# Attention and FFN in one kernel: the hand-over to the FFN re-ordered, with tile 0's reload in four transfers

## The chip, the core and the metric

One Trainium2 chip, one core. The time is the device time of one execution in microseconds, as the median of the runs. The core has TensorE (PE), VectorE (DVE), ScalarE (ACT), GpSimd (POOL) and SyncE (SP), which issues nearly all transfers here. Each engine runs its own program in order; they wait for one another on semaphores.

## What is computed

x has the shape (8, 1024, 512), the context (8, 64, 384); all is float32. Cut to its core:

```python
h = layernorm(x)                                   # over 512 channels, no gain
q, k, v = h @ Wq + bq, ctx @ Wk + bk, ctx @ Wv + bv   # 16 heads of 32
a = softmax(clip(q k^T * 32**-0.5, -1e4, 1e4))     # 64 keys
a = where(any(isnan(a)), 1/64, a)
x = x + (a v) @ Wo + bo
h = layernorm(x) @ W1 + b1                         # 2048 hidden channels
imag = w_imag * sin(theta + 0.1 * h)
h = h + 0.1 * (cos(theta) * w_real + sin(theta) * w_imag) * imag
x = x + relu(h) @ W2 + b2
```

## The kernel before, in words

The 8192 tokens are cut into 16 tiles of 512 (`TILES`), each of four blocks of 128 rows (`NB`). Every engine's program is written out by hand, with a `wait_ge` ahead of each operation that needs another engine. Most products are split: a float32 operand is held as a rounded part (`..._hi`) and the rest (`..._lo`), and `product` issues three matmuls (hi*hi, lo*hi, hi*lo; L1129 to L1131). ACT writes the hi part out of PSUM, DVE subtracts it to get the lo part.

**Phase A, attention.** The loop over `i` (0 to `STEPS_A` - 1 = 69) takes a group of four heads of a tile per step; there are 64 groups (`GROUPS`), four to a tile. At step i PE makes the scores of group i, transposes the probabilities of group i - 2 (`late = i - LAG_A`, L1198 to L1213, into the banks `pt_bank`), makes the queries of group i + 1, one output block y of `n = i - 6` (attention output times Wo, bank `y_bank`) and then the product of probabilities and values of group `late` (bank `o_bank`). Behind the scores of a group stands a chain over three engines: DVE clips (L983) and takes the maximum, POOL subtracts it (L591), ACT takes the exponential, POOL adds halves, DVE sums and inverts, POOL multiplies by the inverse (L586, `prob_done`). The steps 64 to 69 only drain: the last transposes at 64 and 65, the blocks y 58 to 63 at 64 to 69. For each block DVE adds the residual that SP has loaded into `res` (L1039, `y_done`), and SP stores it to the buffer `x1_dram` (L423), then loads the residual three blocks further on (L427) as soon as the store of the block that used the same quarter of `res` has landed. At step 64 PE also makes one small product (L1317), which counts rows without NaN; DVE casts it (`nan_count`), and POOL decides by it and sets `guard_done` (L620), on which SP's reload of finished rows waits.

**The seam.** SP loads tiles 0 and 1 of the attention's result back into `x_sb[0]` and `x_sb[1]` (L437 to L438), inside its loop over the blocks, behind the load for block 60. POOL adds `bo_row` block by block (`add_output_bias`, L555), DVE takes the statistics (`layer_stats`, two blocks at step 67, two at step 68), POOL takes the power -1/2 (`rsqrt`, L521), DVE makes the shifts (`layer_shift`, L869, at step 69), ACT normalises the four blocks into `xn` (L690), PE transposes them (L1135 in `transposes`, into banks 0 to 3), ACT and DVE split the result into `xt_hi` and `xt_lo` (L673, L875), and PE begins the FFN. Ahead of these transposes PE waits for all 64 residual additions (`y_done`, L1336).

**Phase B, FFN.** For each tile 16 hidden chunks f: PE makes the hidden values (banks 0 to 3), ACT, DVE and POOL work out the sine and the activation, PE multiplies chunk f - 3 by W2 into banks 4 to 7 (`second`). In tile 0 ACT and DVE also split the rest of the weights; before the first of these splits they wait until all blocks of `x1_dram` are stored and POOL has set `last_done`. The hidden chunk 1 and those after it follow one another on ACT and DVE through `turns`, `frac`, `hid` and `act`.

Of the kernel before, what the change touches and what calls it, by code (L numbers as in the profile page):

```python
# [15 lines left out]
P = 128  # L16
# [56 lines left out]
def ring(at):  # L73
    return 2 + at % 6
# [15 lines left out]
def y_bank(i):  # L90
    return ring(STEP_AT[i % KC] + 3 + KC * (i % KC == 2))
# [20 lines left out]
def xattn_ffn(nc, x, ctx_768, wq, bq, wk, bk, wv, bv, wo, bo, w1, b1, phases, w_real, w_imag, w2, b2,  # L112
# [6 lines left out]
    with stack:  # L119
# [123 lines left out]
        x0_in = sems("x0_in", NB)  # L243
# [60 lines left out]
        def x_loads(T):  # L304

            return 16 * ((T + 1) // XBUFS)
# [66 lines left out]
        def _(sp):  # L373
# [46 lines left out]
            for n in range(TILES * NB):  # L420
# [13 lines left out]
                if n == NB * GUARDED + 1:  # L434
                    sp.wait_ge(guard_done, 1)
                    sp.wait_ge(xt_psum, KC * TILES)
                    for t in range(XBUFS):  # L437
                        sp.dma_start(x_sb[t][:], x1_rows[t]).then_inc(x_in[t], 16)  # L438
# [41 lines left out]
        def _(pool):  # L480
# [69 lines left out]
            def add_output_bias(t, n):  # L550
                tile = x_sb[t % XBUFS]
                pool.wait_ge(x_in[t % XBUFS], x_loads(TILES + t))
                if t == 0 and n == 0:
                    pool.wait_ge(bias_in, 48)
                pool.tensor_tensor(tile[:, n, :], tile[:, n, :], bo_row[:], ALU.add).then_inc(x1_whole, 1)  # L555
# [68 lines left out]
            rsqrt(TILES)  # L624
            for n in range(NB):
                add_output_bias(1, n)
# [32 lines left out]
        def _(act):  # L659
# [15 lines left out]
            def layer_rows(T, blocks):  # L675
                if T == TILES or T < TILES:
                    if T:
                        act.wait_ge(x_in[T % XBUFS], x_loads(T))
# [167 lines left out]
        def _(dve):  # L846
            def layer_stats(T, blocks):
                if T:
                    dve.wait_ge(x_in[T % XBUFS], x_loads(T))
# [107 lines left out]
            for i in range(STEPS_A):  # L957
# [73 lines left out]
                if i in (STEPS_A - 3, STEPS_A - 2):  # L1031
                    layer_stats(TILES, half_blocks(i - STEPS_A + 3))
                if i == STEPS_A - 1:
                    layer_shift(TILES)
# [90 lines left out]
        def _(pe):  # L1125
# [52 lines left out]

            for i in range(STEPS_A):
# [16 lines left out]
                if 0 <= late < GROUPS:  # L1196

                    pe.wait_ge(prob_done, late + 1)  # L1198
                    for j in range(PAIRS):
                        if late == 0:  # L1200
                            pe.wait_ge(vn_done, 3) if j else pe.wait_ge(kt_done, 1)
                        elif has_burst(i - 1):
                            pe.wait_ge(xt_lo_done, KC * (t + 1) + j + 1)
                        elif j == 0 and late >= 2:
                            pe.wait_ge(o_lo_done, late - 1)
                        else:
                            pe.wait_ge(pt_lo_done, PAIRS * late - 1)
                        for blk in range(NB):
                            heads = slice(blk * HG + 2 * j, blk * HG + 2 * j + 2)
                            m = pe.transpose(psum[:, pt_bank(i, j), blk * P:(blk + 1) * P],  # L1210
                                             prob[:, late % SCORE_BUFS, heads, :].rearrange("p h k -> p (h k)"),
                                             ident[:])
                        m.then_inc(pt_psum, 1)  # L1213
# [54 lines left out]
                if 0 <= n < TILES * NB:  # L1268
# [3 lines left out]
                    if i < GROUPS:  # L1272
                        if g < 2:
                            pe.wait_ge(q_full_done, i + 1)
                        elif g == 2:
                            pe.wait_ge(pt_lo_done, PAIRS * (late + 1))
                    elif i == GROUPS + LAG_A:
# [10 lines left out]
                    m.then_inc(y_psum, 1)  # L1288
                if 0 <= late < GROUPS:
# [30 lines left out]
            def second(j):  # L1320
                t, f = divmod(j, FC)
                if t == 0:
                    pe.wait_ge(w_lo_done, w2_split[f])
                pe.wait_ge(act_lo_done, j + 1)
# [11 lines left out]
            pe.wait_ge(y_done, NB * TILES)  # L1336
# [57 lines left out]
```

## Time and profile before

| | before |
|---|---|
| median of 3 runs | 2078.79 us (2077.18 to 2079.24) |
| the profiled execution: its time, its span | 2078.33 us, 2076.6 us |
| TensorE's mean granted clock | 0.998 of full speed |
| PE busy | 2049.5 us (99%) |
| DVE, ACT, POOL busy | 1354.3, 1145.1, 1041.6 us |

The span is the stretch that the profile covers; the execution's time is 1.7 us more. Times in the rows are microseconds from the start of the span. A row's busy time of a matmul reaches until its result is out, so that matmuls which follow without a pause overlap: the starts of two neighbours, not their busy times, tell what one costs.

### The profile page before, as it was taken

To read this page: it belongs to the slowest core of one execution; us is meant where nothing else is said; L and a number is where in the kernel's file an instruction comes from. 1 tells how busy PE (TensorE), PEld (TensorE's weight loads), DVE (VectorE), ACT (ScalarE), POOL (GpSimd) and SP (SyncE) were. 2 spreads that over 40 slices of the span, in tenths; PEclk is the share of its full clock that TensorE was granted. 3 is DMA by queue.
4 is the path that set the end of the run, shared out by engine and by line. 5 is a ranking of instruction groups with operands and counts; after the bars stand their busy time and mean duration, and the time that the engine had idled before them with its cause. 6 is when DMAs were issued, how large, how long until landed. Compare 5 with 4: busy or idle time off the path is not lost.

```text
span 2076.6 us, 27122 instructions
## 1 busy us (share of the span) xinstructions
PE 2049.5 (99%) x9746; PEld 1715.9 (83%) x9746; DVE 1354.3 (65%) x2024; ACT 1145.1 (55%) x2036; POOL 1041.6 (50%) x757
## 2 busy tenths in 40 slices
PE   7999999999998999999999999999999999999999
PEld 5888888888887888888888888888888888888887
DVE  5888888888876665555555565555656555565554
ACT  4767667666664655454554545544455454554543
POOL 3777777777775245343343533435334353343521
PEclk9999999999999999999999999999999999999999
DMA  5123222222213221211112111121111211112100
GB/s 183 56 78 111 82 94 100 87 102 87 72 52 128 88 71 49 72 41 41 41 51 71 41 41 41 51 72 41 41 41 51 71 41 41 41 46 77 40 22 21
DMA packets 133462, 133.93 MB, mean 64 GB/s; under 512 B 68680, under 2 KB 84552, under 8 KB 133328
## 3 DMA queue, kind: packets, MB, share of 16 engines
q1 hardware_dynamic: 132176, 131.64, 21.2%
q8 instruction: 77, 1.26, 0.3%
q10 hardware_dynamic: 1152, 0.56, 0.1%
q14 instruction: 57, 0.47, 0.1%
HBM read 81.83 MB, written 50.35 MB: 64 GB/s over the span
## 4 chain that ended last, share of the span: by engine, by line
PE 89%; DVE 4%; ACT 2%; issue 2%; DMA 1%; POOL 1%; SPq 0%; POOLq 0%; ACTq 0%; DVEq 0%
PE psum L1129 28%; PE psum L1131 28%; PE psum L1130 28%; PE psum L1210 2%; PE psum L1135 1%; DVE hid L1061 1%; DMA ctx_sb<-in_ctx 0%; DVE prob L983 0%; DVE act_lo L1064 0%; ACT act_hi L813 0%; DMA x_sb<-in_x 0%; DVE top L989 0%; DVE total L969 0%; ACT hid L824 0%; POOL prob L591 0%
## 5 line engine op out<-in xcount | busy, mean ns | idle before, releaser
L642 POOL TENSOR_TENSOR frac<-turns,frac 128x512 f32<-128x512 f32 x256 | 333.4, 1302 | 830.0 <-DVE frac L1089 830.0
L1061 DVE SCALAR_TENSOR_TENSOR hid<-frac,gain,hid 128x512 f32<-128x512 f32 x256 | 322.4, 1259 | 143.6 <-ACT frac L809 142.4
L1129 PE MATMUL psum<-w_hi,act_hi 128*128 128x512 f32 x1024 | 398.4, 389 | 0.9 <-DVE act_lo L1064 0.9
L1130 PE MATMUL psum<-w_lo,act_hi 128*128 128x512 f32 x1024 | 398.3, 389 | 0.0
L1131 PE MATMUL psum<-w_hi,act_lo 128*128 128x512 f32 x1024 | 398.3, 389 | 0.0
L813 ACT ACTIVATE act_hi<-hid 128x512 fp32r<-128x512 f32 x256 | 161.8, 632 | 356.3 <-DVE hid L1061 356.3
L822 ACT ACTIVATE turns<-psum,u_shift 128x512 f32<-128x512 f32 x256 | 176.5, 689 | 327.1 <-PE psum L1131 268.9
L1064 DVE SCALAR_TENSOR_TENSOR act_lo<-hid,act_hi 128x512 fp32r<-128x512 f32 x256 | 197.6, 772 | 178.8 <-ACT act_hi L813 178.8
L1089 DVE TENSOR_SCALAR frac<-turns 128x512 f32<-128x512 f32 x256 | 111.3, 435 | 249.0 <-ACT turns L822 249.0
L1129 PEld LDWEIGHTS psum<-w_hi,act_hi 128*128 128x128 f32 x1024 | 192.3, 188 | 41.2 <-issue 1.2
L1131 PEld LDWEIGHTS psum<-w_hi,act_lo 128*128 128x128 f32 x1024 | 192.2, 188 | 40.0
L1130 PEld LDWEIGHTS psum<-w_lo,act_hi 128*128 128x128 f32 x1024 | 192.1, 188 | 39.8
L1129 PE MATMUL psum<-xt_hi,w1a_hi 128*128 128x512 f32 x512 | 199.6, 390 | 0.0
L1130 PE MATMUL psum<-xt_lo,w1a_hi 128*128 128x512 f32 x512 | 199.4, 389 | 0.0
L1131 PE MATMUL psum<-xt_hi,w1a_lo 128*128 128x512 f32 x512 | 199.2, 389 | 0.0
L1129 PE MATMUL psum<-xt_hi,w1b_hi 128*128 128x512 f32 x512 | 199.2, 389 | 0.0
L1130 PE MATMUL psum<-xt_lo,w1b_hi 128*128 128x512 f32 x512 | 199.2, 389 | 0.0
L1131 PE MATMUL psum<-xt_hi,w1b_lo 128*128 128x512 f32 x512 | 199.2, 389 | 0.0
L586 POOL TENSOR_TENSOR prob<-prob,inv 128x1024 f32<-128x1024 f32 x64 | 122.0, 1906 | 105.5 <-DVE inv L971 105.5
L824 ACT ACTIVATE hid<-psum,par 128x512 f32<-128x512 f32 x256 | 174.5, 682 | 0.0
L809 ACT ACTIVATE frac<-frac 128x512 f32<-128x512 f32 x256 | 161.3, 630 | 0.0
L748 ACT ACTIVATE psum<-psum 128x512 f32<-128x512 f32 x128 | 74.5, 582 | 122.5 <-DVE prob L983 122.5
(149 smaller groups left out, 4178.6 us busy)
## 6 DMA issues: line engine op xcount, KB each, us to landing
res<-in_x SPq DMA_DIRECT2D x64, 256.0 KB, 2.9
x_dram<-res SPq DMA_DIRECT2D x64, 256.0 KB, 2.0
x_sb<-x_dram SPq DMA_DIRECT2D x16, 1024.0 KB, 5.5
x_sb<-in_x SPq DMA_DIRECT2D x15, 1024.0 KB, 5.8
xn<-turn_dram SPq DMA_DIRECT2D x30, 512.0 KB, 5.1
out<-x_sb SPq DMA_DIRECT2D x15, 1024.0 KB, 4.9
turn_dram<-stage SPq DMA_DIRECT2D x112, 128.0 KB, 2.4
stage<-in_w SPq DMA_DIRECT2D x32, 256.0 KB, 2.8
```

Of the source, the lines that this page charges most:

```text
L586: pool.tensor_tensor(rows, rows, inv[:, (i - 1) % 2, :].unsqueeze(2) .to_broadcast([P, NB * HG, KEYS]), ALU.mult).then_inc(prob_done, 1)
L642: pool.tensor_tensor(frac[:, j % 2, :], turns[:, j % 2, :], frac[:, j % 2, :], ALU.subtract)\
L809: act.activation(frac[:, j % 2, :], frac[:, j % 2, :], ACT.Sin, scale=SIN_SCALE).then_inc(sin_done, 1)
L813: act.activation(act_hi[:, j % ACTS, :], hid[:, j % 2, :], ACT.Relu).then_inc(act_hi_done, 1)
L822: act.activation(turns[:, j % 2, :], hidden, ACT.Identity, bias=u_shift[:, f:f + 1], scale=0.1 / TWO_PI).then_inc(turns_done, 1)
L824: act.activation(hid[:, j % 2, :], hidden, ACT.Identity, bias=par[:, 3, f:f + 1])\
L1061: dve.scalar_tensor_tensor(out=hid[:, j % 2, :], in0=frac[:, j % 2, :], scalar=gain[:, f:f + 1], in1=hid[:, j % 2, :], op0=ALU.mult, op1=A ...
L1064: dve.scalar_tensor_tensor(out=act_lo[:, j % ACTS, :], in0=hid[:, j % 2, :], scalar=0.0, in1=act_hi[:, j % ACTS, :].bitcast(F32), op0=ALU. ...
L1089: dve.tensor_scalar(frac[:, j % 2, :], turns[:, j % 2, :], ROUND, ROUND, ALU.add, ALU.subtract)\
L1129: pe.matmul(o, a_hi, b_hi, start=first, stop=False)
L1130: pe.matmul(o, a_hi, b_lo, start=False, stop=False)
L1131: return pe.matmul(o, a_lo, b_hi, start=False, stop=last)
```

## The change

Six edits, all around the seam:

1. The transposes of the probabilities become a function `transpose_rows(i)`. Those of the last group (63) are called at step 64 behind the block y, no longer at step 65 ahead of it. Their waits are the same.
2. Block y of step 62 (n = 56) goes to bank 5, no longer to bank 7, and waits there for `o_lo_done` of group 59; before, it waited for both lo parts of the probabilities of group 60 (`pt_lo_done`).
3. Tile 0's reload is four transfers of a block each, with four semaphores `x1_in`; POOL adds the bias to a block when that block is in. ACT and DVE need no wait of their own for this load, and have none.
4. DVE takes the statistics of all four blocks and the shifts at step 67, ahead of the residual additions of blocks 61, 62 and 63.
5. POOL waits for these shifts before it adds the bias to tile 1.
6. PE's wait for `y_done` moves from ahead of the first FFN transposes to ahead of the first product with W2.

```diff
 def y_bank(i):
-    return ring(STEP_AT[i % KC] + 3 + KC * (i % KC == 2))
+    return ring(STEP_AT[i % KC] + 3 + (2 if i == GROUPS - 2 else KC) * (i % KC == 2))
...
-            return 16 * ((T + 1) // XBUFS)
+            return 16 * ((T + 1) // XBUFS - (T >= TILES and T % XBUFS == 0))
...
-                    for t in range(XBUFS):
-                        sp.dma_start(x_sb[t][:], x1_rows[t]).then_inc(x_in[t], 16)
+                    for blk1 in range(NB):
+                        sp.dma_start(x_sb[0][:, blk1, :], x1_rows[0][:, blk1, :]).then_inc(x1_in[blk1], 16)
+                    sp.dma_start(x_sb[1][:], x1_rows[1]).then_inc(x_in[1], 16)
...
             def add_output_bias(t, n):
                 tile = x_sb[t % XBUFS]
-                pool.wait_ge(x_in[t % XBUFS], x_loads(TILES + t))
+                if t:
+                    pool.wait_ge(x_in[t % XBUFS], x_loads(TILES + t))
+                else:
+                    pool.wait_ge(x1_in[n], 16)
...
             rsqrt(TILES)
+            pool.wait_ge(shift_rows_done, TILES + 1)
             for n in range(NB):
                 add_output_bias(1, n)
...
-                if T == TILES or T < TILES:
-                    if T:
-                        act.wait_ge(x_in[T % XBUFS], x_loads(T))
+                if 0 < T < TILES:
+                    act.wait_ge(x_in[T % XBUFS], x_loads(T))
...
-                if T:
+                if T and T != TILES:
                     dve.wait_ge(x_in[T % XBUFS], x_loads(T))
...
-                if i in (STEPS_A - 3, STEPS_A - 2):
-                    layer_stats(TILES, half_blocks(i - STEPS_A + 3))
-                if i == STEPS_A - 1:
+                if i == STEPS_A - 3:
+                    layer_stats(TILES, range(NB))
                     layer_shift(TILES)
...
-                if 0 <= late < GROUPS:
-
-                    pe.wait_ge(prob_done, late + 1)
...
+                if 0 <= late < GROUPS - 1:
+                    transpose_rows(i)
...
-                        elif g == 2:
+                        elif has_burst(i):
                             pe.wait_ge(pt_lo_done, PAIRS * (late + 1))
+                        elif i == GROUPS - 2:
+                            pe.wait_ge(o_lo_done, late)
...
+                if i == GROUPS:
+                    transpose_rows(i + 1)
                 if 0 <= late < GROUPS:
...
+                if j == 0:
+                    pe.wait_ge(y_done, NB * TILES)
                 pe.wait_ge(act_lo_done, j + 1)
...
             pe.wait_ge(nan_count, 1)
-            pe.wait_ge(y_done, NB * TILES)
             pe.wait_ge(xn_done, TILES + 1)
```

How the instructions stand on the engines. PE in step 64 and at the start of step 65, before; `pt`, `vbd` is the product with the values, `row_ok` the NaN count, `wo` a block y, and `[waits ...]` names the semaphores:

```order
L1131 MATMUL psum<-wo_hi,o_lo 128x512
L1129 MATMUL psum<-pt_hi,vbd_hi 128x512 [waits pt_lo_done,y_done]
L1130 MATMUL psum<-pt_lo,vbd_hi 128x512
L1131 MATMUL psum<-pt_hi,vbd_lo 128x512
L1129 MATMUL psum<-pt_hi,vbd_hi 128x512 [waits pt_lo_done]
L1130 MATMUL psum<-pt_lo,vbd_hi 128x512
L1131 MATMUL psum<-pt_hi,vbd_lo 128x512
L1317 MATMUL psum<-ones,row_ok 1x1 [waits nan_step]
L1210 MATMUL psum<-ident,prob 128x128 [waits o_lo_done,prob_done]
L1210 MATMUL psum<-ident,prob 128x128 x3
L1210 MATMUL psum<-ident,prob 128x128 [waits pt_lo_done]
L1210 MATMUL psum<-ident,prob 128x128 x3
```

The same place after the change:

```order
L1134 MATMUL psum<-wo_hi,o_lo 128x512
L1197 MATMUL psum<-ident,prob 128x128 [waits o_lo_done,prob_done]
L1197 MATMUL psum<-ident,prob 128x128 x3
L1197 MATMUL psum<-ident,prob 128x128 [waits pt_lo_done]
L1197 MATMUL psum<-ident,prob 128x128 x3
L1132 MATMUL psum<-pt_hi,vbd_hi 128x512 [waits pt_lo_done,y_done]
L1133 MATMUL psum<-pt_lo,vbd_hi 128x512
L1134 MATMUL psum<-pt_hi,vbd_lo 128x512
L1132 MATMUL psum<-pt_hi,vbd_hi 128x512 [waits pt_lo_done]
L1133 MATMUL psum<-pt_lo,vbd_hi 128x512
L1134 MATMUL psum<-pt_hi,vbd_lo 128x512
L1328 MATMUL psum<-ones,row_ok 1x1 [waits nan_step]
```

The eight transposes of the last group now stand ahead of the six matmuls with the values of group 62 and of the NaN count.

DVE from step 66 to the FFN's first lo parts, before; `res` is a residual addition (blocks 60 to 63), `mv` and `var_eps` end the statistics:

```order
L1039 TENSOR_TENSOR res<-psum,res 128x512
L857 BN_STATS stats<-x_sb0 128x6 x2
L1039 TENSOR_TENSOR res<-psum,res 128x512
L857 BN_STATS stats<-x_sb0 128x6 x2
L861 BN_AGGR mv<-stats 128x2 x4
L864 TENSOR_SCALAR var_eps<-mv 128x4
L1039 TENSOR_TENSOR res<-psum,res 128x512
L869 SCALAR_TENSOR_TENSOR shift_rows<-mv,rstd 128x4
L1039 TENSOR_TENSOR res<-psum,res 128x512
L875 TENSOR_TENSOR xt_lo<-psum,xt_hi 128x512 x4
```

After the change:

```order
L1042 TENSOR_TENSOR res<-psum,res 128x512
L861 BN_STATS stats<-x_sb0 128x6 x4
L865 BN_AGGR mv<-stats 128x2 x4
L868 TENSOR_SCALAR var_eps<-mv 128x4
L873 SCALAR_TENSOR_TENSOR shift_rows<-mv,rstd 128x4
L1042 TENSOR_TENSOR res<-psum,res 128x512 x3
L879 TENSOR_TENSOR xt_lo<-psum,xt_hi 128x512 x4
```

Three residual additions that stood between and behind the statistics now stand behind the shifts.

SP's issues around the reload; `x_sb0` and `x_sb1` are tiles 0 and 1, and the rows around them the store and the load of the blocks in the loop:

```order
@@ -155,6 +155,6 @@
 L423 DMA x1_dram<-res 128x512
 L427 DMA res<-in_x 128x512
-L438 DMA x_sb0<-x1_dram 128x4x512
-L438 DMA x_sb1<-x1_dram 128x4x512
+L438 DMA x_sb0<-x1_dram 128x512 x4
+L439 DMA x_sb1<-x1_dram 128x4x512
 L423 DMA x1_dram<-res 128x512
```

One issue has become four, so the store of block 58 and all behind it on this queue stand three issues further back.

## Rows read from the trace of the kernel before

**Rows 1.** PE at the seam, timeline: start, busy, operation [idle before] (us)
```profile
637.87 0.50 PE L1129 MATMUL psum<-wo_hi,o_hi 128*128 128x512 f32 x1 [0.92 <-DVE pt_lo L995]
...
653.54 0.47 PE L1129 MATMUL psum<-pt_hi,vbd_hi 128*128 128x512 f32 x1 [0.59 <-DVE pt_lo L995]
...
655.20 1.09 PE L1210 MATMUL psum<-ident,prob 128*128 128x128 f32 x8
...
670.89 0.39 PE L1131 MATMUL psum<-wo_hi,o_lo 128*128 128x512 f32 x1
675.62 3.18 PE L1135 MATMUL psum<-ident,xn 128*128 128x128 f32 x16 [4.34 <-ACT xn L690]
...
679.73 0.39 PE L1129 MATMUL psum<-xt_hi,w1a_hi 128*128 128x512 f32 x1
```

**Rows 2.** The timeline of DVE at the seam
```profile
663.23 0.69 DVE L1039 TENSOR_TENSOR res<-psum,res 128x512 f32<-128x512 f32 x1 [1.47 <-PE psum L1131]
...
667.61 0.69 DVE L1039 TENSOR_TENSOR res<-psum,res 128x512 f32<-128x512 f32 x1 [2.34 <-DMA res<-in_x]
...
669.53 0.38 DVE L861 BATCH_NORM_AGGREGATE mv<-stats 128x2 f32<-128x6 f32 x4
...
671.25 1.22 DVE L869 SCALAR_TENSOR_TENSOR shift_rows<-mv,rstd 128x4 f32<-128x4 f32 x1 [0.53 <-POOL rstd L521]
...
679.47 0.69 DVE L875 TENSOR_TENSOR xt_lo<-psum,xt_hi 128x512 fp32r<-128x512 f32 x1 [0.16 <-ACT xt_hi L673]
```

**Rows 3.** The timeline of POOL at the seam
```profile
652.41 1.91 POOL L586 TENSOR_TENSOR prob<-prob,inv 128x1024 f32<-128x1024 f32 x1 [1.09 <-DVE inv L971]
656.22 0.10 POOL L620 MEMSET ones<- 128x1 f32 x1 [1.90 <-DVE ok_count L1030]
662.00 5.04 POOL L555 TENSOR_TENSOR x_sb<-x_sb,bo_row 128x512 f32<-128x512 f32 x4 [5.68 <-DMA x_sb<-x_dram]
670.19 1.02 POOL L521 TENSOR_TENSOR rstd<-var_eps,minus_half 128x4 f32<-128x4 f32 x1 [3.15 <-DVE var_eps L864]
```

**Rows 4.** The timeline of ACT at the seam
```profile
642.28 0.60 ACT L796 ACTIVATE o_hi<-psum 128x512 fp32r<-128x512 f32 x1 [2.67 <-PE psum L1131]
...
672.55 2.93 ACT L690 ACTIVATE xn<-x_sb,shift_rows,rstd 128x512 f32<-128x512 f32 x4 [9.88 <-issue]
```

**Rows 5.** The timeline of SP, which issues the transfers
```profile
656.35 0.93 SPq L438 DMA_DIRECT2D x_sb<-x_dram  x2
...
666.03 0.33 SPq L427 DMA_DIRECT2D res<-in_x  x1
...
668.20 0.33 SPq L427 DMA_DIRECT2D res<-in_x  x1
```

**Rows 6.** The loads of x_sb (L438), then of res (L427): issue to landing
```profile
DMA to landing us min/median/max: 5.6/7.1/8.6
...
DMA to landing us min/median/max: 2.8/2.9/9.7
```

**Rows 7.** The windows behind the long wait: busy us by engine, PEclk, DMA
```profile
675.60:680.00 4.40, 4.38 (x21) 4.12 (x22) 2.61 (x4) 2.39 (x4) 0.57 (x2) 0.61 0.11 33
```

**Rows 8.** The chain that ended last, from FFN tile 0 to tile 1
```profile
684.44 0.24 PE psum L1131
684.71 0.69 ACT turns L822
...
764.58 0.47 PE psum L1129
```

**Rows 9.** The program's first microseconds, with tile 0's four loads
```profile
0.80 1.81 SPq L397 DMA_DIRECT2D x_sb<-in_x  x4
...
9.34 0.69 DVE L857 BATCH_NORM_STATS2 stats<-x_sb 128x6 f32<-128x512 f32 x1 [1.27 <-DMA x_sb<-in_x]
...
11.87 0.16 DVE L869 SCALAR_TENSOR_TENSOR shift_rows<-mv,rstd 128x4 f32<-128x4 f32 x1 [1.22 <-POOL rstd L521]
```

More of the change, by code:

```diff
@@ L242, in xattn_ffn @@
         x_in = sems("x_in", XBUFS)
-        x0_in = sems("x0_in", NB)
+        x0_in, x1_in = sems("x0_in", NB), sems("x1_in", NB)
         res_in, x1_stored = sems("res_in", NB), sems("x1_stored", NB)
@@ L1177, in _, with transpose_rows @@
             values(0)
+            def transpose_rows(i):
+                t, late = i // KC, i - LAG_A
+                pe.wait_ge(prob_done, late + 1)
+                for j in range(PAIRS):
+                    if late == 0:
+                        pe.wait_ge(vn_done, 3) if j else pe.wait_ge(kt_done, 1)
+                    elif has_burst(i - 1):
+                        pe.wait_ge(xt_lo_done, KC * (t + 1) + j + 1)
+                    elif j == 0 and late >= 2:
+                        pe.wait_ge(o_lo_done, late - 1)
+                    else:
+                        pe.wait_ge(pt_lo_done, PAIRS * late - 1)
+                    for blk in range(NB):
+                        heads = slice(blk * HG + 2 * j, blk * HG + 2 * j + 2)
+                        m = pe.transpose(psum[:, pt_bank(i, j), blk * P:(blk + 1) * P],
+                                         prob[:, late % SCORE_BUFS, heads, :].rearrange("p h k -> p (h k)"),
+                                         ident[:])
+                    m.then_inc(pt_psum, 1)
             for i in range(STEPS_A):
@@ L1195, in _ @@
                             m.then_inc(s_psum, 1)
-                if 0 <= late < GROUPS:
-                    pe.wait_ge(prob_done, late + 1)
[L1199 to L1213, printed above, removed]
+                if 0 <= late < GROUPS - 1:
+                    transpose_rows(i)
                 if i + 1 < GROUPS:
```

## The prediction

> **What bounds the kernel now.** I read the page first. PE is busy for 99% of the span and the other engines for at most 65%, and the chain that ended last lies on PE for most of its length, so only time in which PE stands still or runs slowly can be won. Then PE's timeline, for its pauses. The largest within the program is the seam: the last matmul of the last block y starts at 670.89, and the first FFN transpose starts at 675.62, behind a wait of 4.34 us for ACT's `xn` [rows 1]. Behind it PE is slow as well. The window from 675.60 to 680.00 has a granted clock of 0.61, a mean of its two levels, 2.4 GHz (1.00) and 1.2 GHz (0.50), and the second trio of FFN products (the first matmul that runs at the full pace again) starts at 679.73, so 16 transposes and three matmuls took 4.11 us [rows 1, 7]. Two smaller pauses lie ahead of it: 0.92 us in front of block y 56, and 0.59 us in front of the values of group 62, both for `pt_lo` [rows 1].
>
> Then what is late at the seam, backwards. ACT normalises from 672.55, for 2.93 us [rows 4]. It waits for DVE's shifts, which start at 671.25 and take 1.22 us; these wait for POOL's power (670.19, 1.02 us) and this for the statistics, whose last part starts at 669.53 [rows 2, 3]. The statistics are late because DVE stood for 2.34 us, until 667.61, in front of a residual addition whose load had not landed [rows 2]. POOL's four bias additions run from 662.00 to 667.04, behind a wait of 5.68 us for the reload that SP issued at 656.35 [rows 3, 5]. So two things make `xn` late: a reload that counts only as a whole, and residual additions ahead of the statistics in DVE's order.
>
> **The tail of attention (edits 1 and 2).** Block y 56 no longer waits for `pt_lo`; the group 59 that it now waits for is two groups back. PE is 0.92 us ahead from there. The softmax chain of group 63 follows, since ACT's copy in front of it waited for PE (2.67 us idle, until 642.28) [rows 4]. POOL's last multiplication, 652.41 + 1.91 = 654.32, thus ends at 653.40 [rows 3]. PE reaches the moved transposes when block y 58 is issued: 653.54 - 0.59 = 652.95 before, 652.03 now [rows 1]. It waits there for the probabilities, 653.40 - 652.03 = 1.37 us. Removed are 0.92 + 0.59 = 1.51, added 1.37: I take a gain of 0.1. Bounds: if POOL's chain doesn't move up, PE waits 2.29 and loses 0.8; if the pause were hidden it would gain 1.5. It is a trade of one stall for another, because the probabilities aren't there earlier.
>
> Queued behind the moved transposes are the values of group 62 and the NaN count. Eight transposes cost some 0.9 (busy 1.09 with the result's way out [rows 1]), so these values start near 654.4, where they started at 653.54, and the count with them is 0.8 to 0.9 later. On the count hang `guard_done` (656.22) and the reload (656.35) [rows 3, 5]: it goes out at about 657.2. This is the price of edit 1 for the seam. The values of group 63 have 0.2 us to spare by my count of ACT's and DVE's copies (0.6 to 0.7 us each, one behind the other, under the 12 matmuls of block y 59); a miss costs a few tenths.
>
> **The seam (edits 3, 4, 5).** A transfer of 256 KB of the same shape takes 2.8 to 2.9 us where nothing is in its way [rows 6], so the first quarter lands at 657.2 + 2.9 = 660.1. POOL's four additions, 5.04 us [rows 3], then end at 665.1, if the other quarters come at least every 1.26 us, the last by 663.9. The whole first megabyte took 5.6 us [rows 6], which would be 662.8, plus what three more issues of 0.47 us cost [rows 5]; so they should. DVE is free after block 60's addition at 663.23 + 0.69 = 663.9 [rows 2]. The fourth statistics end at 665.1 + 0.7 = 665.8, the rest of them at 666.4 (0.38 us [rows 2], and a small addition), POOL's power at 667.5 (1.02 [rows 3]), the shifts at 667.7, ACT at 667.7 + 2.93 = 670.7 [rows 4]. PE's last block y is issued by 670.89 + 0.23 - 0.1 = 671.0 [rows 1, 8]. `xn` comes 0.3 ahead of that: the pause closes. The transposes start at 671.1, where they started at 675.62.
>
> The shifts took 1.22 us beside POOL's additions for tile 1, and 0.16 us at the start of the program [rows 2, 9]; edit 5 keeps POOL still, and I take 0.2. If they still took 1.22, `xn` would be ready at 671.7 and 0.3 to 0.7 us would be lost. The Trainium skill (GPSIMD Engine Reference, Specifications) says that GpSimd's SBUF interfaces are shared with VectorE, with contention for DVE instructions with two SBUF inputs, as this one has. By that rule it is the short one, by 1.06 us; the trace agrees.
>
> **What is late next.** Without the pause the clock has no reason in this trace to fall: it stood at full through pauses of 0.92 and 0.59 us and fell only behind the one of 4.34 [rows 1, 7]. At full pace 16 transposes take 1.75 (twice the eight) and three matmuls 0.68. But `xt_lo` now stands in DVE's queue behind three residual additions, of which the last needs the load of block 63. That load waited for a store and was issued at 668.20 [rows 5]; the bytes in front of it are the same and start 0.8 later, so 669.0, and it lands at 671.9. Addition and first `xt_lo` take 0.69 each [rows 2]: 673.3, and the trio behind them ends its issue at 674.0. That is 679.73 - 674.0 = 5.7 us earlier than before. Without the late load it would be 671.1 + 2.43 = 673.5, a gain of 6.2; with the slow clock nevertheless, 671.1 + 4.11 = 675.2, a gain of 4.5.
>
> **Is it kept?** From 684.71 to 764.58 the chain that ended last runs over ACT and DVE, not PE: the first FFN tile, in which they split weights too [rows 8]. It hangs on PE's hidden chunk 1, issued at 684.44 [rows 8], so it starts earlier with PE, by the same 5.7. Two things in it don't hang on PE. The last block must be stored: added by 672.6, landed near 676. POOL must have passed `last_done`: four additions behind the shifts, 667.7 + 5.0 = 672.7. ACT asks for both some 1.6 us before `turns` of chunk 1 (two copies of weights of about 0.6 us, and a short pause), so at 684.7 - 5.7 - 1.6 = 677.4. Both are in, the store with about 1 us to spare. Behind tile 0 nothing changes. Edit 6 by itself costs nothing: by the first product with W2 all additions are long over.
>
> **Sum.** 0.1 + 4.4 (pause) + 1.2 (clock, less the late load) = 5.7 us. The profiled execution took 2078.33, 1.7 more than its span, and goes to 2072.6; the median of the runs lies 0.46 above that execution, so 2073.1.
>
> **The rivals.**
>
> *The quarters come late.* At the start of the program four such quarters were issued from 0.80 on, and the statistics of the fourth waited until 9.34, 8.5 us [rows 9]; other loads followed close behind, as here tile 1's megabyte does. So the last quarter lands at 665.8, its bias ends at 667.1, `xn` at 672.7. The pause is 1.7, the gain 2.9 plus up to 1.7 of clock: 2074.2 to 2075.9. At the worst the four land together with the last, 657.2 + 5.6 + 1.4 = 664.2, and POOL's 5.04 follow: `xn` at 674.9, the gain 0.7, 2078.1. The Trainium skill speaks against the split (DMA: Bandwidth & Descriptors, Rules for kernel authors: at least 1 MiB per DMA for bandwidth); by it this rival is the case. For it speaks the start, against it the quiet queue ahead of this reload, and that 256 KB loads take 2.9. Chance 0.20, a third of it with a gain over 4.2.
>
> *The gain is lost behind the seam or in the tail.* The clock falls at the new pause of 1.4 us (a stretch of some 4 us at half pace costs 2), or the store of the last block holds the chain in tile 0. Gain 2.5 to 4: 2074.8 to 2076.3. Chance 0.11.
>
> *Slower.* The load of block 63 is now ahead of `xt_lo`. One load of `res` took 9.7 us [rows 6]. Issued at 669.0 that is 678.7, with 1.4 of DVE and 0.7 of PE 680.8, against 679.73 before: 1 us slower, 2079.9. It decides from a landing at 677.6 on. Against it: that load had two megabytes in front of it, which are through by 666. Chance 0.03; over 0.2% slower would need 4 us more, hence I leave 0.02 for that.
>
> *The forecast*, 2071.8 to 2074.5: chance 0.66.
>
> **How the numbers follow.** 0.2% is 4.2 us, about what a measurement of this kernel can tell. Faster by more: 0.66 and a third of 0.20, 0.72. Slower 0.02, the same 0.26. The range goes from 2071.6 (the gain of 6.2 and some more in the tail) to 2076.5, which takes in the late quarters and most of the losses.
>
> **What would show it.** Block y 56 starts straight behind the queries. The transposes of group 63 wait near 1.4 us for POOL. POOL's first bias addition begins near 660 and has no long pauses after it. The shifts take about 0.2 and come before three additions. The FFN's transposes have no pause over 0.5 in front, and the granted clock behind them is full. The first `xt_lo` comes near 672.6. The prediction is wrong if POOL waits between its four additions, if PE's clock is under full at 654 or 672, or if the chain in tile 0 begins at something other than PE.

## The result, and the profile after

| | before | changed |
|---|---|---|
| median of 11 runs | 2077.4 us (2075.13 to 2079.24) | 2072.85 us (2071.2 to 2075.03) |
| ratio to before, 95% interval | | 0.998 (0.9971 to 0.9989) |
| the profiled execution: time, span | 2078.33, 2076.6 us | 2072.03, 2070.3 us |
| PE busy | 2049.5 us | 2047.8 us |

The change makes the kernel faster by 0.2%: 4.2 us by the ratio (2.3 to 6.0), 4.55 us by the medians. The forecast was 2073.1 us, a gain of 5.7.

The two profiled executions differ by 6.3 us of span, and not all of it is the change. The start of the program, which the change doesn't touch, happened to be quicker: the residual addition of block 55 on DVE starts at 630.64 before and at 629.99 after. So times of the two traces are compared as distances from this addition. Two distances are used from here on: to the first FFN transpose on PE (44.98 us before, 40.34 after), and to ACT's `turns` of hidden chunk 1, at which the chain through FFN tile 0 begins (54.07 before, 48.64 after); the recorded expectations call this second distance the yardstick. The seam is thus 5.43 us shorter; from `turns` of chunk 1 to the end of the span it is 1391.9 us before and 1391.7 after.

The timeline of PE in the changed kernel, around the seam (start, busy, operation, idle before), which answers to [rows 1]:

```profile
652.49 1.09 PE L1197 MATMUL psum<-ident,prob 128*128 128x128 f32 x8 [1.41 <-POOL prob L590]
...
669.89 0.39 PE L1134 MATMUL psum<-wo_hi,o_lo 128*128 128x512 f32 x1
670.33 1.94 PE L1138 MATMUL psum<-ident,xn 128*128 128x128 f32 x16
672.87 0.47 PE L1132 MATMUL psum<-xt_hi,w1a_hi 128*128 128x512 f32 x1 [0.61 <-DVE xt_lo L879]
...
673.65 0.39 PE L1132 MATMUL psum<-xt_hi,w1a_hi 128*128 128x512 f32 x1
```

The wait of 4.34 us for `xn` is gone; the transposes follow the last block y with no pause that the view lists. New are 1.41 us ahead of the moved transposes, for POOL's last multiplication, and 0.61 us ahead of the first FFN product, for the first `xt_lo`. The 16 transposes take 1.94 us instead of 3.18. A window over this stretch shows why (columns: the stretch, its length, busy time and count of PE, PEld, DVE, ACT and POOL, then the granted clock, the DMA share and GB/s):

```profile
671.00:674.00 3.00, 2.39 (x17) 2.01 (x16) 2.56 (x5) 2.06 (x4) 1.36 (x3) 1.00 0.68 255
```

It is at 1.00, 2.4 GHz, where [rows 7] had 0.61. The timeline of DVE, for [rows 2]:

```profile
662.23 0.69 DVE L1042 TENSOR_TENSOR res<-psum,res 128x512 f32<-128x512 f32 x1 [1.47 <-PE psum L1134]
662.83 2.46 DVE L861 BATCH_NORM_STATS2 stats<-x_sb 128x6 f32<-128x512 f32 x4
665.33 0.38 DVE L865 BATCH_NORM_AGGREGATE mv<-stats 128x2 f32<-128x6 f32 x4
...
667.05 0.16 DVE L873 SCALAR_TENSOR_TENSOR shift_rows<-mv,rstd 128x4 f32<-128x4 f32 x1 [1.13 <-POOL rstd L522]
667.95 0.69 DVE L1042 TENSOR_TENSOR res<-psum,res 128x512 f32<-128x512 f32 x1 [0.74 <-DMA res<-in_x]
...
671.43 0.69 DVE L1042 TENSOR_TENSOR res<-psum,res 128x512 f32<-128x512 f32 x1 [1.50 <-DMA res<-in_x]
672.04 2.47 DVE L879 TENSOR_TENSOR xt_lo<-psum,xt_hi 128x512 fp32r<-128x512 f32 x4
```

All four statistics run in one piece, the shifts take 0.16 us and start at 667.05, and only then the three residual additions come. The last of them, of block 63, waited 1.50 us for its load, and the first `xt_lo` stands right behind it. The statistics begin when DVE is done with block 60's addition, not when POOL is done: they end at 665.29, and POOL's last bias addition (below) ended at 664.01. POOL, for [rows 3]:

```profile
650.54 1.90 POOL L590 TENSOR_TENSOR prob<-prob,inv 128x1024 f32<-128x1024 f32 x1 [1.09 <-DVE inv L975]
656.04 0.10 POOL L624 MEMSET ones<- 128x1 f32 x1 [3.60 <-DVE ok_count L1034]
658.95 5.06 POOL L559 TENSOR_TENSOR x_sb<-x_sb,bo_row 128x512 f32<-128x512 f32 x4 [2.81 <-DMA x_sb<-x_dram]
666.00 1.02 POOL L522 TENSOR_TENSOR rstd<-var_eps,minus_half 128x4 f32<-128x4 f32 x1 [1.99 <-DVE var_eps L868]
```

POOL waits 2.81 us for the first quarter, where it waited 5.68 for the whole tile, and makes its four additions without a pause. ACT, for [rows 4, 8], and SP, for [rows 5]:

```profile
667.25 2.94 ACT L694 ACTIVATE xn<-x_sb,shift_rows,rstd 128x512 f32<-128x512 f32 x4 [5.58 <-DVE shift_rows L873]
...
678.63 0.69 ACT L826 ACTIVATE turns<-psum,u_shift 128x512 f32<-128x512 f32 x1 [0.41 <-PE psum L1134]
```

```profile
656.17 1.75 SPq L438 DMA_DIRECT2D x_sb<-x_dram  x4
...
668.63 0.33 SPq L427 DMA_DIRECT2D res<-in_x  x1
```

### The profile page after: what moved, and what is told of

Same layout as the page of the kernel before. It is cut to its first block, busy times and chain, and to the rows that moved or that the text cites. A ratio compares the mean times of both kernels' runs of the same rounds, so it can differ in the third digit from the quotient of the medians.

```text
span 2070.3 us, 27125 instructions
## 1 busy us (share of the span) xinstructions
PE 2047.8 (99%) x9746; PEld 1715.1 (83%) x9746; DVE 1353.3 (65%) x2024; ACT 1144.8 (55%) x2036; POOL 1041.0 (50%) x757
## 4 chain that ended last, share of the span: by engine, by line
PE 90%; DVE 4%; ACT 2%; DMA 1%; issue 1%; POOL 1%; SPq 0%; ACTq 0%; DVEq 0%; POOLq 0%
PE psum L1132 29%; PE psum L1134 29%; PE psum L1133 28%; PE psum L1197 2%; PE psum L1138 1%; DVE hid L1064 1%; DMA x_dram<-res 0%; DMA ctx_sb<-in_ctx 0%; ACT act_hi L817 0%; DVE act_lo L1067 0%; DMA x_sb<-in_x 0%; DVE prob L987 0%; ACT hid L828 0%; DVE top L993 0%; POOL prob L595 0%
```

## The experiments

Each experiment was profiled and timed against the kernel before on the same chip. A microsecond is 0.05%, less than the half-width of the intervals of the ratios (about 0.1%), so the small steps are read from the traces, by the two distances. Each distance is of one execution.

| run | block 55's addition | first FFN transpose | `turns` of chunk 1 | first distance | second distance | median, ratio (95% interval) |
|---|---|---|---|---|---|---|
| before | 630.64 | 675.62 | 684.71 | 44.98 | 54.07 | |
| changed | 629.99 | 670.33 | 678.63 | 40.34 | 48.64 | 2072.85, 0.998 (0.9971 to 0.9989) |
| e1: edit 1 undone | 630.61 | 670.11 | 678.06 | 39.50 | 47.45 | 2071.53, 0.9973 (0.9961 to 0.9984) |
| e11: the same again | 631.30 | 670.78 | 679.84 | 39.48 | 48.54 | 2071.53, 0.9977 (0.9966 to 0.9987) |
| e2: edit 3 undone | 628.21 | 670.83 | 679.87 | 42.62 | 51.66 | 2075.44, 0.9994 (0.9984 to 1.0003) |
| e3: edit 4 undone | 630.17 | 675.08 | 684.71 | 44.91 | 54.54 | 2077.33, 1.0003 (0.9994 to 1.0013) |
| e4: edit 6 undone | 629.44 | 672.93 | 680.87 | 43.49 | 51.43 | 2074.89, 0.9996 (0.9986 to 1.0006) |
| e5: edit 5 undone | 631.39 | 672.82 | 681.31 | 41.43 | 49.92 | 2071.05, 0.9976 (0.9964 to 0.9987) |
| e6: tile 1 loaded later | 627.77 | 668.16 | 677.87 | 40.39 | 50.10 | 2072.12, 0.9978 (0.9968 to 0.9988) |
| e7: first lo parts ahead of block 63 | 629.49 | 669.83 | 677.78 | 40.34 | 48.29 | 2071.83, 0.9976 (0.9966 to 0.9985) |
| e8: before, with edit 2 alone | 629.76 | 672.79 | 681.77 | 43.03 | 52.01 | 2075.18, 0.9992 (0.9983 to 1.0002) |
| e9: e1, NaN count earlier | 629.97 | 669.18 | 677.13 | 39.21 | 47.16 | 2070.28, 0.9968 (0.9956 to 0.9981) |
| e10: e9, part of block y 59 earlier | 627.69 | 666.43 | 674.35 | 38.74 | 46.66 | 2069.61, 0.9968 (0.9956 to 0.998) |
| e12: changed, NaN count earlier | 630.46 | 670.47 | 678.41 | 40.01 | 47.95 | 2071.32, 0.9972 (0.9962 to 0.9982) |

Of the experiments that undo an edit, only the interval of e3 (edit 4) lies clear of the changed kernel's; those of e2 and e4 overlap it slightly. For edits 1 and 5 the times show nothing: e1, e11 and e5 are as fast as the changed kernel or faster.

**e1 and e11: is edit 1 part of the gain?** The transposes of the last group go back to step 65:

```diff
-                if 0 <= late < GROUPS - 1:
+                if 0 <= late < GROUPS:
                     transpose_rows(i)
...
-                if i == GROUPS:
-                    transpose_rows(i + 1)
```

> The changed kernel with edit 1 undone: the transposes of the last group stand at step 65 again, ahead of block y 59; all else as changed. Yardstick for all experiments: from the start of the residual addition of block 55 on DVE to the start of ACT's turns of hidden chunk 1. Before 54.07 us, changed 48.64 us. Theory (edit 1 trades one stall for a longer one: PE stands 1.41 us for the probabilities where it stood 0.59 us for pt_lo): with it undone PE stands about 0.4 to 0.6 us in front of the values of group 62 and not at all in front of the transposes, the FFN's transposes come 0.8 to 0.9 us earlier, the reload 1.7 us earlier, yardstick 47.3 to 47.9. Rival (the move belongs to the gain, its cover for pt_lo is needed further on): yardstick 49.2 or more.

The timeline of PE in e1:

```profile
652.31 0.47 PE L1132 MATMUL psum<-pt_hi,vbd_hi 128*128 128x512 f32 x1 [0.63 <-DVE pt_lo L999]
...
653.97 1.09 PE L1197 MATMUL psum<-ident,prob 128*128 128x128 f32 x8
...
670.11 1.94 PE L1138 MATMUL psum<-ident,xn 128*128 128x128 f32 x16
672.30 0.47 PE L1132 MATMUL psum<-xt_hi,w1a_hi 128*128 128x512 f32 x1 [0.25 <-DVE xt_lo L879]
```

Two groups of heads behind each other, PE stands 0.63 us for `pt_lo`, and the transposes find their probabilities ready. The first distance is 0.84 us shorter, in both executions (39.50 and 39.48): 1.41 - 0.63 = 0.78 of it is this stall. The reload leaves SP 24.50 us behind block 55's addition (655.11 - 630.61), where it was 26.18 in the changed kernel, 1.7 us earlier. The theory holds for the stall. For the second distance (47.3 to 47.9 expected) it holds in e1, with 47.45, and not in e11, with 48.54:

> The kernel of the first experiment again, beside the two above on the same chip: yardstick 47.3 to 47.6, time 0.996 to 0.9985 of before.

The timeline of PE in e11, and DVE's addition of block 63 in e1 and in e11:

```profile
674.11 0.47 PE L1132 MATMUL psum<-xt_hi,w1a_hi 128*128 128x512 f32 x1 [1.39 <-DVE xt_lo L879]
```

```profile
670.42 0.69 DVE L1042 TENSOR_TENSOR res<-psum,res 128x512 f32<-128x512 f32 x1 [1.67 <-DMA res<-in_x]
```

```profile
672.67 0.69 DVE L1042 TENSOR_TENSOR res<-psum,res 128x512 f32<-128x512 f32 x1 [1.91 <-DMA res<-in_x]
```

The first FFN product waited 1.39 us for `xt_lo` here, 0.25 in e1, with the same instructions. The difference is the load of block 63, which was issued 1.25 us later (37.97 against 36.72 us behind block 55) and took 0.3 longer from issue to use (3.40 against 3.09). So edit 1 costs 0.84 us up to the transposes, in both executions. In the second distance its whole price, the stall and the later reload, is 1.19 us against e1 and only 0.10 against e11, where the load was as late as in the changed kernel (41.37 us behind block 55's addition, 41.44 there) although the reload had gone out earlier. By time the kernels can't be told apart: e1 and e11 have 0.9973 and 0.9977, the changed one 0.998.

**e2: what the four transfers are worth.**

```diff
-                    for blk1 in range(NB):
-                        sp.dma_start(x_sb[0][:, blk1, :], x1_rows[0][:, blk1, :]).then_inc(x1_in[blk1], 16)
+                    sp.dma_start(x_sb[0][:], x1_rows[0]).then_inc(x1_in[0], 16)
...
-                    pool.wait_ge(x1_in[n], 16)
+                    pool.wait_ge(x1_in[0], 16)
```

> The changed kernel with edit 3 undone: tile 0 is reloaded in one transfer of 1 MB, and POOL's four bias additions wait for it as a whole. Theory (the quarters let POOL begin 2.8 us after the issue, not 5.6): POOL begins 2.5 to 2.8 us later, the statistics end 2.2 us later, the FFN's transposes wait some 2 us for xn, yardstick 48.64 + 1.5 to 2.2 = 50.1 to 50.8, and up to 1.3 more if the granted clock falls behind this pause. Rival (the late load of block 63 in front of the first xt_lo sets the end anyway, the quarters give nothing): 48.6 to 49.0.

POOL and PE in e2, and a window behind PE's pause:

```profile
660.04 5.04 POOL L558 TENSOR_TENSOR x_sb<-x_sb,bo_row 128x512 f32<-128x512 f32 x4 [5.67 <-DMA x_sb<-x_dram]
```

```profile
670.83 3.54 PE L1137 MATMUL psum<-ident,xn 128*128 128x128 f32 x16 [2.33 <-ACT xn L693]
```

```profile
672.00:673.00 1.00, 1.00 (x7) 1.00 (x6) 0.36 (x1) 0.79 (x2) 0.82 (x2) 0.50 0.61 121
```

POOL waits 5.67 us again, PE 2.33, and the granted clock is 0.50 in the midst of the transposes, which take 3.54 us instead of 1.94. The second distance is 3.02 us longer: 2.28 in the pause (first distance), the rest the clock, less the late load, which the pause hides. The theory's figure with a fallen clock, 50.1 to 52.1, holds; the rival (48.6 to 49.0) is out.

**e3: the order on DVE.**

```diff
-                if i == STEPS_A - 3:
-                    layer_stats(TILES, range(NB))
+                if i in (STEPS_A - 3, STEPS_A - 2):
+                    layer_stats(TILES, half_blocks(i - STEPS_A + 3))
+                if i == STEPS_A - 1:
                     layer_shift(TILES)
```

> The changed kernel with edit 4 undone: two blocks' statistics at step 67, two at step 68, the shifts at step 69, with the residual additions between. Theory (the residual additions, which wait for loads behind the reload, held the statistics): the statistics end some 4 us later, the transposes wait 4 us for xn, yardstick 52.4 to 53.8, nearly the whole gain gone. Rival (the quarters alone made xn early, the order on DVE hardly matters): at most 49.6.

DVE and PE in e3:

```profile
668.17 0.69 DVE L1043 TENSOR_TENSOR res<-psum,res 128x512 f32<-128x512 f32 x1 [3.85 <-DMA res<-in_x]
```

```profile
675.08 3.65 PE L1139 MATMUL psum<-ident,xn 128*128 128x128 f32 x16 [4.60 <-ACT xn L694]
```

DVE stands 3.85 us in front of block 61's addition, with the second half of the statistics behind it, although the quarters came early. The second distance is 54.54, nothing left of the gain, 0.7 more than the theory's upper end: the load of block 61 is held by the reload and comes later than I had it. The quarters without the order are worth nothing, and the order without the quarters (e2) is worth 54.07 - 51.66 = 2.4 us, of which edit 2 alone gives 2.06 (e8, below). They need each other. Beside e8, which keeps the old reload and order, e3 is even 2.53 us slower: the load of block 61 is issued 3.0 us later (29.02 against 26.03 us behind block 55's addition), 1.7 of it since the reload goes out later, as edit 1 makes it do, and 1.3 since there are three more issues ahead of it on SP.

**e4: the wait for all additions ahead of the transposes.**

```diff
+            pe.wait_ge(y_done, NB * TILES)
             pe.wait_ge(xn_done, TILES + 1)
...
-                if j == 0:
-                    pe.wait_ge(y_done, NB * TILES)
```

> The changed kernel with edit 6 undone: PE waits for all 64 residual additions ahead of the first FFN transposes. Theory: the addition of block 63 ends 1.8 us behind the point at which the transposes can start now, so they start 1.9 us later; xt_lo stands behind the same addition anyway, so the hidden chunks come only about 1.3 us later: yardstick 49.8 to 50.1. Rival (edit 6 is worth nothing, since xt_lo has the same wait in DVE's order): 48.6 to 48.8.

PE in e4, and a window in its transposes:

```profile
672.93 1.94 PE L1138 MATMUL psum<-ident,xn 128*128 128x128 f32 x16 [3.19 <-DVE res L1042]
675.12 0.47 PE L1132 MATMUL psum<-xt_hi,w1a_hi 128*128 128x512 f32 x1 [0.25 <-DVE xt_lo L879]
```

```profile
673.00:674.00 1.00, 1.00 (x10) 1.00 (x11) 0.00 (x0) 0.34 (x1) 0.00 (x0) 1.00 0.31 117
```

The transposes start 3.15 us later, not 1.9, and `turns` 2.79 later, not 1.3. The direction is the theory's, the size for `turns` twice as large (51.43 against 49.8 to 50.1), and the rival (48.6 to 48.8) is out: the addition of block 63 came 42.70 us behind block 55's here, 41.44 in the changed kernel, so some 1.3 us of the 2.8 is the unsteady load. Edit 6 is worth 1.5 us with the load as it was in the changed kernel, more when the load is late. PE's pause of 3.19 us left the clock at 1.00, where the one of 2.33 in e2 brought it down.

**e5: POOL's wait for the shifts.**

```diff
-            pool.wait_ge(shift_rows_done, TILES + 1)
```

> The changed kernel with edit 5 undone: POOL goes on from the power to tile 1's bias additions without waiting for DVE's shifts. Theory (this small DVE instruction with two SBUF inputs is held while POOL's addition runs): the shifts take about 1.2 us instead of 0.16, the transposes start 1.0 us later, yardstick 48.64 + 0.4 to 0.6 = 49.0 to 49.3 since the late load of block 63 hides the rest. Rival (the 1.22 us before came of something else): shifts 0.16 to 0.3 us, yardstick 48.6.

DVE and POOL in e5:

```profile
668.46 1.25 DVE L872 SCALAR_TENSOR_TENSOR shift_rows<-mv,rstd 128x4 f32<-128x4 f32 x1 [1.13 <-POOL rstd L522]
```

```profile
668.40 5.00 POOL L559 TENSOR_TENSOR x_sb<-x_sb,bo_row 128x512 f32<-128x512 f32 x4
```

The shifts take 1.25 us again when POOL's additions start beside them, and the first distance grows by 1.09. The second grew by 1.28, above the 0.4 to 0.6 expected, since the load of block 63 was late here as well (42.72 us). The rival is out. The Trainium skill (GPSIMD Engine Reference, Specifications) names contention for DVE instructions with two SBUF inputs; this run agrees with it. The times don't show this loss: e5's median is 2071.05 us, and the profiled execution, with 2074.72, was the slowest of its seven.

**e6 and e7: the late load of block 63.** In e6 SP issues tile 1's reload behind the load of block 63; in e7 DVE makes the first `xt_lo` ahead of the addition of block 63.

```diff
-                    sp.dma_start(x_sb[1][:], x1_rows[1]).then_inc(x_in[1], 16)
+                if n == NB * GUARDED + 4:
+                    sp.dma_start(x_sb[1][:], x1_rows[1]).then_inc(x_in[1], 16)
```

```diff
                 if 0 <= n < TILES * NB:
+                    if n == TILES * NB - 1:
+                        for k in range(KC):
+                            xt_to_lo(TILES, k, k)
                     dve.wait_ge(res_in[n % NB], 16 * (n // NB + 1))
```

> The changed kernel, but SP issues the reload of tile 1 three blocks later, behind the load for block 63. Theory (the store of block 59 and so the load of block 63 were late because a megabyte for tile 1 stood ahead of them): this load lands before PE is done with block 63, PE's pause of 0.61 us in front of the first FFN product shrinks to about 0.1, yardstick 48.0 to 48.2; tile 1's bias additions begin near the time of the shifts or 1 to 2 us later and hold nothing. Rivals: the four quarters alone keep the stores back, 48.6; or tile 1's late bias additions hold last_done and with it the weight splits of the first FFN tile, 49 or more.

> The changed kernel, but DVE makes the four first xt_lo of the FFN ahead of the residual addition of block 63. Theory (only this addition, waiting for its load, kept the first xt_lo back): PE's pause of 0.61 us goes to about 0.1, yardstick 48.0 to 48.2; the store of block 63 goes out some 2.5 us later and is still in time for the weight splits, or just holds them (then 48.4 to 49). Rival (xt_lo is held by ACT's copies, not by the addition): 48.6.

PE and ACT in e6, then in e7:

```profile
670.35 0.47 PE L1133 MATMUL psum<-xt_hi,w1a_hi 128*128 128x512 f32 x1 [0.25 <-DVE xt_lo L880]
```

```profile
676.80 0.63 ACT L675 ACTIVATE w_hi<-stage 128x512 fp32r<-128x512 f32 x1 [2.14 <-POOL ones L642]
```

```profile
672.02 0.47 PE L1132 MATMUL psum<-xt_hi,w1a_hi 128*128 128x512 f32 x1 [0.26 <-DVE xt_lo L879]
```

```profile
676.52 0.64 ACT L674 ACTIVATE w_hi<-stage 128x512 fp32r<-128x512 f32 x1 [0.19 <-issue]
```

In both the pause in front of the first product is 0.25 us, so the rest of the 0.61 was the addition of block 63 and its load. In e6 tile 1's megabyte was late in turn: POOL passed `last_done` only at 676.51, ACT stood 2.14 us in front of the first weight split, and the second distance is 1.46 longer in spite of the earlier product, 50.10 where 48.0 to 48.2 was expected. That is the second rival. In e7 0.35 us are won; 48.29 is just above the 48.0 to 48.2 expected. ACT stands 0.19 us in front of the split there. The view names no releaser; POOL had passed `last_done` at 671.76, so most likely it is the store of block 63, the other thing that it waits for here.

**e8: edit 2 alone, on the kernel before.**

```diff
-    return ring(STEP_AT[i % KC] + 3 + KC * (i % KC == 2))
+    return ring(STEP_AT[i % KC] + 3 + (2 if i == GROUPS - 2 else KC) * (i % KC == 2))
...
-                        elif g == 2:
+                        elif has_burst(i):
                             pe.wait_ge(pt_lo_done, PAIRS * (late + 1))
+                        elif i == GROUPS - 2:
+                            pe.wait_ge(o_lo_done, late)
```

> The kernel before with edit 2 alone: block y 56 in bank 5, without its wait for pt_lo. Theory (the softmax chain of group 63 hangs on PE, so it moves up with it): the pauses of 0.4 and 0.59 us stay, everything behind comes 0.9 to 1.2 us earlier, the reload and all of the seam with it, yardstick 54.07 - 1.1 = 52.8 to 53.2. Rival (the chain over DVE, POOL and ACT keeps its own time and PE just waits elsewhere): 54.0.

PE in e8, and the starts around the pause of 0.92 us before:

```profile
651.44 0.47 PE L1129 MATMUL psum<-pt_hi,vbd_hi 128*128 128x512 f32 x1 [0.59 <-DVE pt_lo L995]
...
672.79 3.47 PE L1135 MATMUL psum<-ident,xn 128*128 128x128 f32 x16 [3.59 <-ACT xn L690]
```

```profile
636.56 0.39 PE L1131 MATMUL psum<-xt_hi,wq_lo 128*128 128x512 f32 x1
637.87 0.50 PE L1129 MATMUL psum<-wo_hi,o_hi 128*128 128x512 f32 x1 [0.92 <-DVE pt_lo L995]
638.21 0.40 PE L1130 MATMUL psum<-wo_lo,o_hi 128*128 128x512 f32 x1
```

The pause of 0.92 is gone and that of 0.59 is as long as it was, so the softmax chain follows PE, as the theory says. From block 55's addition to block 56's it is 9.13 us, where it was 10.35, so the pause had cost 1.22. The view counts it only from the end of the last result; by the starts, the two matmuls around it are 1.31 us apart where neighbours have 0.23, and the next one comes 0.34 behind. The second distance fell by 2.06, more than the 0.9 to 1.3 expected (52.8 to 53.2) and 0.84 more than the pause; the rest came in the seam, where block 61's addition waited 1.43 us for its load instead of 2.34.

**e9, e10 and e12: a better version.** The NaN count's product moves ahead of the values of group 62 (in e12, ahead of the moved transposes; in e9 with edit 1 undone); e10 also moves the first three matmuls of block y 59 there.

```diff
+                if i == GROUPS:
+                    pe.wait_ge(nan_step, 2)
+                    pe.matmul(psum[0:1, 0, 0:1], row_ok[:], ones[:], start=True, stop=True).then_inc(nan_psum, 1)
                 if 0 <= late < GROUPS:
...
-                if i == GROUPS:
-                    pe.wait_ge(nan_step, 2)
-                    pe.matmul(psum[0:1, 0, 0:1], row_ok[:], ones[:], start=True, stop=True).then_inc(nan_psum, 1)
```

In e10, in addition:

```diff
-                    for k in range(KC):
+                    for k in range(1 if i == GROUPS + 1 else 0, KC):
...
+                if i == GROUPS:
+                    slot, toks = (n + 1) // NB * KC % O_BUFS, slice((n + 1) % NB * P, ((n + 1) % NB + 1) * P)
+                    product(psum[:, y_bank(i + 1), :], (o_hi[:, slot, toks], o_lo[:, slot, toks]),
+                            (wo_hi[:, 0, :], wo_lo[:, 0, :]), True, False)
```

> The kernel of the first experiment (changed, edit 1 undone), and the NaN count's product ahead of the values of group 62, right behind block y 58. Yardsticks so far: before 54.07, changed 48.64, edit 1 undone 47.45. Theory (what is left of the seam is PE's own work, 0.25 us for the first xt_lo and some 0.2 us in front of the transposes, where xn is just late): the reload goes out 1.5 to 2 us earlier, xn is early, the loads of blocks 62 and 63 are early, yardstick 47.1 to 47.3. Rival (the pause for pt_lo moves, or DVE's order holds the count): 47.45 or more.

> The kernel of e9_count_up, and the first three matmuls of block y 59 (0.68 us) moved up a step into PE's pause of 0.6 us in front of the values of group 62. Theory: the pause goes, all behind it comes 0.6 us earlier, yardstick 0.5 to 0.6 less than that of e9_count_up, near 46.6. Rival: the values of group 63 then wait for their pt_lo, since block y 59 covers that wait with nine matmuls only, yardstick as e9_count_up.

> The changed kernel, edit 1 kept, with the NaN count's product ahead of the moved transposes. It parts the price of edit 1: the stall on PE (about 0.8 us) and the later reload. Theory: the reload goes out 3 to 3.9 us earlier, the load of block 63 is in time, PE's pause in front of the first FFN product shrinks from 0.61 to 0.25, yardstick 48.64 - 0.35 - 0.0 to 0.2 = 48.1 to 48.3; the rest to 47.45 is the stall. Rival (the late load of block 63 has nothing to do with the time of the reload): 48.6.

PE in e10, in e12, and POOL in e12:

```profile
651.02 1.04 PE L1197 MATMUL psum<-ident,prob 128*128 128x128 f32 x8
...
666.43 1.94 PE L1138 MATMUL psum<-ident,xn 128*128 128x128 f32 x16
668.62 0.47 PE L1132 MATMUL psum<-xt_hi,w1a_hi 128*128 128x512 f32 x1 [0.25 <-DVE xt_lo L879]
```

```profile
652.96 1.09 PE L1197 MATMUL psum<-ident,prob 128*128 128x128 f32 x8 [1.30 <-POOL prob L590]
...
672.67 0.47 PE L1132 MATMUL psum<-xt_hi,w1a_hi 128*128 128x512 f32 x1 [0.26 <-DVE xt_lo L879]
```

```profile
653.39 0.10 POOL L624 MEMSET ones<- 128x1 f32 x1 [0.49 <-issue]
656.30 5.07 POOL L559 TENSOR_TENSOR x_sb<-x_sb,bo_row 128x512 f32<-128x512 f32 x4 [2.80 <-DMA x_sb<-x_dram]
```

e12: the reload goes out 3.1 us earlier (653.52 - 630.46 = 23.06, after 26.18), the load of block 63 is in time, the pause in front of the first product is 0.26 and the second distance 47.95, a little under the 48.1 to 48.3 expected. Of the 0.69 us won, 0.35 is this pause; the other 0.33 is in the first distance, and block 60's addition is earlier by as much already (31.91 against 32.24 us behind block 55's), so it is won on PE and not by the reload. From e12 to e9 it is 0.79, the stall. e9 has 47.16 and e10 46.66, as expected: the view of PE shows no pause in front of the values of group 62 any more. e10's median is 2069.61, its ratio 0.9968 (0.9956 to 0.998), 6.6 us under the kernel before (4.2 to 9.1). Against the changed kernel the traces give 1.98 us; the intervals of the ratios (0.9956 to 0.998 and 0.9971 to 0.9989) overlap.

## Why the prediction was right

The time, the sign and the mechanism hold. The gain was forecast at 5.7 us; the traces of the two executions show 5.43 in the seam, the runs 4.2 (2.3 to 6.0). That the time itself was met to 0.25 us (2073.1 against 2072.85) is in part luck: the gain by medians was 1.15 us short of the forecast, and the kernel before has 2077.4 in eleven runs where the forecast set out from 2078.79 in three, 1.39 more. The times below are the prediction's, put on the changed execution's axis by taking off the 0.65 us that its start was quicker.

- **The tail.** POOL's last multiplication was to follow PE: it ends at 652.44 (forecast 652.75). PE was to stand 1.37 us for it; it stood 1.41. The removed pause was worth 1.22, not 0.92 (e8). The net gain in the tail is 0.35 us (the last matmul of block y: 669.89 + 0.65 = 670.54 against 670.89), not 0.1.
- **Edit 1 as a trade.** This step was the weakest. The prediction set the new stall against the sum of two old ones, 1.51 us, and found them nearly even. But edit 2 removes the one by itself, so edit 1 trades 0.6 us for 1.4, at a loss of 0.84 up to the transposes (e1, e11). Its other price, the later reload, was seen: 0.8 to 0.9 later than before was forecast; measured from block 55's addition it is 26.18 against 25.71 before, 0.5 later, since the tail in between gained.
- **The seam.** First bias addition at 659.5, shifts done at 667.1, `xn` done at 670.1, transposes at 670.5: measured 658.95, 667.21, 670.19, 670.33. The shifts took 0.16 us (0.2 taken), and e5 shows the cause. One link was other than forecast, and the errors happened to balance. The prediction let POOL's last addition set the end of the statistics; in the trace POOL was done 0.4 us ahead of the forecast, and DVE's own four statistics, which start right behind block 60's addition and take 2.46 us, set it. In all eight executions with edits 3 to 6 in place (the changed kernel, e1, e11, e6, e7, e9, e10, e12) the transposes start 8.10 to 8.13 us behind block 60's addition, whether the reload went out 23.1 or 26.2 us behind block 55's. So in the changed kernel the reload no longer sets the start of the transposes; in e2 it still does.
- **The clock.** Full behind the closed pause, as forecast; the transposes and the first trio took 673.65 - 670.33 = 3.3 us instead of 4.11. e2 shows the half clock behind a pause. The term of the sum for the clock, less the late load, was 1.2 us and came out at 5.43 - 4.64 = 0.79, since the forecast had only 2.9 us for this stretch. Its figure without the late load, 2.43, was too small as well: e1, with an early load, took 2.97 (670.11 to 673.08), for the first product waits 0.25 us for `xt_lo` there too. The tail and the pause were together 0.14 more than forecast (4.64 against 4.5).
- **What is late next.** The load of block 63 was forecast to be issued at 668.4 and to land at 671.3; it was issued at 668.63 and its addition started at 671.43. The first trio's end of issue, forecast 673.4, was 673.65. This is the most exposed step of the sum: in e3, e4 and e5 the addition of block 63 came 1.3 to 1.4 us later than in the changed kernel, and in e11 1.6 later than in e1, the same program, for reasons that these traces don't tell.
- **Kept through tile 0.** From `turns` of chunk 1 to PE's pause at the tile's end it is 79.63 us, after 79.87. The spare time of the two other conditions was real but thin: e6 and e7 used it up.
- **The rivals.** The quarters did not come like those at the start of the program; POOL had no pause between them, though pauses of 0.2 to 0.8 show in e5, e6 and e10. e2, with the megabyte whole, is 3.0 us slower in the seam; what counts here is when the first quarter can be used, not the rate. The rule of the Trainium skill (DMA: Bandwidth & Descriptors, Rules for kernel authors), at least 1 MiB per DMA for bandwidth, didn't decide. The slower case, a load of 9.7 us for block 63, did not occur: it took 2.8.

The gain by runs is 1.2 us below that by traces. The interval of the runs covers both, so nothing follows from it.

## What to carry to other kernels

When a change removes one wait and adds another, price each edit against the kernel with the other edits in place, not against the kernel before: an edit that looks even in the sum can be a loss beside one that does its work alone. At a hand-over between phases, walk the whole chain back to the earliest condition: here early quarters without the new order on DVE gave nothing, moving one tiny product up won 0.7 us (e12), and moving eight transposes up lost 0.8 on the way to the FFN's transposes (e1, e11). And when a pause is closed, look at what stands in the queue behind the thing it waited for; here a late load moved from behind the pause to the front.

## What the hardware showed

- PE's granted clock doesn't go by the length of the pause alone: it was 0.50 behind a pause of 2.33 us (e2) and 1.00 behind one of 3.19 us (e4).
- The load of block 63, 256 KB, was used between 2.8 and 4.1 us after its issue where DVE stood waiting for it (changed 2.8, e1 3.1, e2 and e11 3.4, e3, e4 and e5 4.1). e1 and e11 are the same program; the others differ in what else was under way.
- A pause costs PE more than the idle time that the view lists: with one of 0.92 us gone, the stretch was 1.22 us shorter (e8).
- A DVE instruction on 128x4 elements took 0.16 us by itself and 1.25 beside POOL's addition (changed, e5).
